# Query weight of a cross-attention kernel loaded in runs of 32 channels and transposed by VectorE instead of TensorE

## What is computed

```python
query = hidden_states @ Wq                 # x: 2 x 2048 x 640, f32
keyt, valt = enc @ Wk, enc @ Wv            # enc: 124 tokens of 384 channels
hs = _mha(query, keyt, valt)
ca_q1 = jnp.einsum('btc,th->bch', ca, Wq_ca)[:, indices, :]   # ca: 4 tokens
ca_hs1 = _mha(ca_q1, residual, residual)   # attends to x itself
ca_hs2 = _mha(ca_hs1 @ Wq, ca @ Wk_ca, ca @ Wv_ca)
out = (hs + ca_hs2) @ Wout + b_out + residual
```

## Time and profile before

| | |
|---|---|
| median of three runs | 768.8 us (767.13 to 770.88) |
| the profiled execution, its own time | 769.75 us |
| its span in the trace | 768.0 us |
| TensorE busy | 725.4 us, 94% of the span |
| VectorE busy | 564.1 us, 73% |
| ScalarE busy | 375.9 us, 49% |
| mean granted TensorE clock | 0.982 of full speed |

### The profile page before, as it was taken

The page is one execution under the profiler, slowest core; times in us unless marked ns, Lnnn a source line. Parts: engine busy times, 40 slices in busy tenths (PEclk is TensorE's granted clock), DMA queues, the critical chain, the costliest instruction groups (busy, mean ns, idle before and its releaser), DMA issues.

```text
span 768.0 us, 12603 instructions
## 1 busy us (share of the span) xinstructions
PE 725.4 (94%) x4693; PEld 677.1 (88%) x4693; DVE 564.1 (73%) x952; ACT 375.9 (49%) x942; POOL 171.4 (22%) x205
## 2 busy tenths in 40 slices
PE   7998999999899996968999999999999999799998
PEld 5978999999788886968899999999978887699997
DVE  3456888888899997436674888888889998656562
ACT  1634544454588962222333544455479994142330
POOL 8024951222100003502210521111110002211220
PEclk9999999999999999888999999999999999899999
DMA  8424353333400046697754334444230005578852
GB/s 275 144 94 124 69 125 90 90 90 90 145 30 1 0 76 157 137 218 183 151 139 101 65 90 109 102 98 94 90 129 2 0 1 128 131 159 188 177 124 74
DMA packets 227021, 82.37 MB, mean 107 GB/s; under 512 B 208324, under 2 KB 210372, under 8 KB 226960
## 3 DMA queue, kind: packets, MB, share of 16 engines
q1 hardware_dynamic: 226960, 81.56, 43.4%
HBM read 50.06 MB, written 31.39 MB: 106 GB/s over the span
## 4 chain that ended last, share of the span: by engine, by line
PE 80%; DVE 8%; SPq 3%; DMA 3%; issue 3%; ACT 2%; POOL 0%; DVEq 0%; POOLq 0%
PE PS L1230 30%; PE PS L1435 13%; PE PS L1418 6%; PE PS L1205 6%; PE PS L1305 6%; PE PS L1336 6%; PE PS L1327 5%; PE PS L1177 2%; SPq L432 2%; PE PS L1142 2%; DMA exT<-p_kept 2%; DVE pT_lo L1047 1%; SPq L479 1%; DVE res L1063 1%; PE PS L1188 1%
## 5 line engine op out<-in xcount | busy, mean ns | idle before, releaser
L1230 PE MATMUL PS<-mm_hi,xT_hi 128*128 128x280 f32 (+3 forms) x480 | 159.5, 332 | 0.0
L890 DVE TENSOR_REDUCE mpart<-PS 128x4 f32<-128x512 f32 x192 | 131.6, 687 | 36.9 <-PE PS L1205 36.7
L1230 PE MATMUL PS<-mm_hi,xT_lo 128*128 128x280 f32 (+3 forms) x480 | 157.4, 328 | 0.0
L1230 PE MATMUL PS<-mm_lo,xT_hi 128*128 128x280 f32 (+3 forms) x480 | 156.5, 326 | 0.0
L560 POOL TENSOR_TENSOR ex<-ex,rinv 128x992 f32<-128x992 f32 x30 | 55.4, 1845 | 201.5 <-DVE rinv L884 201.4
L666 ACT ACTIVATE ex<-PS,neg 128x124 f32<-128x124 f32 x256 | 89.9, 364 | 11.7 <-DVE gs L872 6.4
L1230 PEld LDWEIGHTS PS<-mm_hi,xT_hi 128*128 128x128 f32 x480 | 90.2, 188 | 0.7 <-issue 0.5
L1230 PEld LDWEIGHTS PS<-mm_lo,xT_hi 128*128 128x128 f32 x480 | 90.4, 188 | 0.3
L1230 PEld LDWEIGHTS PS<-mm_hi,xT_lo 128*128 128x128 f32 x480 | 90.3, 188 | 0.3
L754 ACT ACTIVATE oT_hi<-PS 128x256 fp32r<-128x256 f32 x80 | 29.5, 384 | 121.7 <-PE PS L1418 121.1
L608 POOL TENSOR_TENSOR xin<-xin,bias 128x640 f32<-128x640 f32 x32 | 49.8, 1562 | 160.6 <-DMA xin<-in_x 160.6
(11 more groups left out here) (154 smaller groups left out, 1355.9 us busy)
## 6 DMA issues: line engine op xcount, KB each, us to landing
ex_kept<-ex SPq DMA_DIRECT2D x32, 512.0 KB, 2.9
ex<-ex_kept SPq DMA_DIRECT2D x112, 128.0 KB, 3.1
xin<-in_x SPq DMA_DIRECT2D x128, 80.0 KB, 2.9
xin<-in_x SPq DMA_DIRECT2D x32, 320.0 KB, 3.5
out<-res SPq DMA_DIRECT2D x32, 320.0 KB, 2.3
raw_kept<-raw SPq DMA_DIRECT2D x5, 512.0 KB, 2.6
ex<-ex_kept SPq DMA_DIRECT2D x4, 512.0 KB, 3.8
mm_lo<-raw_kept SPq DMA_DIRECT2D x10, 186.0 KB, 4.4
```

What stands on the lines that cost most here:

```text
L890: nc.vector.tensor_reduce(mpart[:, n // 2, :, 2 * (n % 2):2 * (n % 2) + 2, i].rearrange("p s k -> p k s"), PS[:, 6 + N % 2, :].rearrange(" ...
L1230: last = mul(PS[:, slot(T, k), p0:p0 + w], l[:, i % 2, j, :], rr[:, m0:m0 + w], start=(j == 0 and n == 0), stop=(n == 2), skip_group_check ...
```

## The change

The query weight is no longer transposed on TensorE. It is loaded by fifteen transfers, three for each block j of 128 channels of the first axis: each takes 32 channels t, the four groups c of 32 inside the block, all eight heads, and a run of 32 head channels (128 bytes; the third run of a head has 16, so 64 bytes). Each transfer has 32 x 8 x 4 = 1024 pieces. `wq_in` is now `[96, 5, 8, 4, 32]`, and VectorE transposes one block j at a time, 96 partitions x 1024 elements, into `wqT[0:96]`. The unused part of the third run is set to zero by one memset at the start of VectorE's list. Blocks 0 to 2 are transposed before the copies to `kT`, block 3 after step m = 1 and block 4 after step m = 5. The 40 transposes of L1159, the eight copies of L633 and the waits between them go. `wkca` is issued after the three transfers of block 0, and tile 0 of x after all fifteen.

```diff
@@ SP @@
-            for f in range(2):
-                sp.dma_start(wq_in[:, :, f * HALF:(f + 1) * HALF], wq[:, f * HALF:(f + 1) * HALF].rearrange("(j p) n -> p j n", p=P))\
-                    .then_inc(wq_in_s[f], 16)
-                if f == 0:
+            for j in range(KT):
+                rows = wq[j * P:(j + 1) * P, :].rearrange("(c t) (h d) -> t h c d", c=4, h=NH)
+                for d in range(3):
+                    w = min(32, D - d * 32)
+                    sp.dma_start(wq_in[d * 32:(d + 1) * 32, j, :, :, 0:w], rows[:, :, :, d * 32:d * 32 + w]).then_inc(wq_in_s[j], 16)
+                if j == 0:
                     sp.dma_start(wk_in[:, 1], wkca.rearrange("(c p) n -> p c n", p=P)).then_inc(wkca_in_s, 16)
@@ ScalarE @@
-            for h in range(NH):
-                act.wait_ge(wqT_ps, h + 1)
-                nc.scalar.activation(wqT[0:D, h, :], flat(2 * (h % 2))[0:D, 0:H], ACT.Copy).then_inc(wqT_made, 1)
@@ VectorE @@
+            def query_blocks(j):
+
+                dve.wait_ge(wq_in_s[j], 3 * 16)
+                nc.vector.transpose(wqT[0:3 * 32, :, j * P:(j + 1) * P], wq_in[:, j].rearrange("t h c k -> t h (c k)")).then_inc(wqT_made, 1)
+            nc.vector.memset(wq_in[2 * 32:3 * 32, :, :, :, 16:32].rearrange("t j h c k -> t (j h c) k"), 0.0).then_inc(wq_zero, 1)
...
+            dve.wait_ge(wq_zero, 1)
+            for j in range(3):
+                query_blocks(j)
             for m in range(NH // 2):
                 dve.wait_ge(kT_ps, m + 1)
...
                 nc.vector.tensor_copy(ca0[:, 2 * m:2 * m + 2, :], ps[:, :, 0, NK:P]).then_inc(ca0_made, 1)
+                if m in (1, 5):
+                    query_blocks(3 + m // 5)
@@ TensorE @@
             pe.wait_ge(wca_made, 1)
+            pe.wait_ge(wkca_in_s, 16)
             for h in range(NH):
-                if h % R == 0:
-                    pe.wait_ge(wq_in_s[h // R], 16)
-                if h >= 2:
-                    pe.wait_ge(wqT_made, h - 1)
-                if h == 1:
-                    pe.wait_ge(aTm_made, R)
-                for j in range(KT):
-                    last = nc.tensor.transpose(flat(2 * (h % 2))[0:D, j * P:(j + 1) * P], wq_in[:, j, h * D:(h + 1) * D], ident[:, :])
-                last.then_inc(wqT_ps, 1)
-                if h == 0:
-                    pe.wait_ge(wkca_in_s, 16)
                 last = kT_part(h, 1, NK, P)
                 if h % 2:
                     last.then_inc(kT_ps, 1)
+            pe.wait_ge(aTm_made, R)
             for m in range(4 * KT):
                 j, h = m // 4, 2 * (m % 4)
-                if m == 0:
-                    pe.wait_ge(wqT_made, NH)
+                if m % 4 == 0:
+                    pe.wait_ge(wqT_made, max(3, j + 1))
```

More of the change, by code:

```diff
@@ L199, in build @@
             with (nc.sbuf_tensor("wk_in", [P, 2, CT, H], F32) as wk_in,
-                  nc.sbuf_tensor("wq_in", [P, KT, H], F32) as wq_in, nc.sbuf_tensor("wqca_in", [NT, H], F32) as wqca_in,
+                  nc.sbuf_tensor("wq_in", [3 * 32, KT, NH, 4, 32], F32) as wq_in, nc.sbuf_tensor("wqca_in", [NT, H], F32) as wqca_in,
                   nc.sbuf_tensor("v_ca", [B * NT, H], F32) as v_ca):
@@ L327, in build @@
                                                             sem("wout_loaded"))
-        wq_in_s = [sem("wq_loaded0"), sem("wq_loaded1")]
+        wq_in_s, wq_zero = [sem("wq_loaded0"), sem("wq_loaded1"), sem("wq_loaded2"), sem("wq_loaded3"), sem("wq_loaded4")], sem("wq_zero")
         bias_in = sem("bias_loaded")
         wca_ps, wca_made, ctxT_ps, ctxT_made, caT_made = sem("wca_ps"), sem("wca_made"), sem("ctxT_ps"), sem("ctxT_made"), sem("caT_made")
-        kT_ps, kT_made, wqT_ps, wqT_made = sem("kT_ps"), sem("kT_made"), sem("wqT_ps"), sem("wqT_made")
+        kT_ps, kT_made, wqT_made = sem("kT_ps"), sem("kT_made"), sem("wqT_made")
         raw_ps, raw1_made, mmh_made, mml_made, ca0_made = sem("raw_ps"), sem("raw1_made"), sem("mmh_made"), sem("mml_made"), sem("ca0_made")
```

## The result

The changed kernel takes 782.64 us (median of four runs, 781.65 to 784.75), against 769.4 for the kernel before in the same comparison. The ratio is 1.018, with a 95% interval from 1.015 to 1.021: 1.8% slower, where 0.57% faster was forecast. The profiled execution took 781.65 us with a span of 779.9, 11.9 us longer than before.

What follows compares the result with a forecast made beforehand. TensorE's setup chain from keys to folding was taken as the bound: 4.45 us gained there, less 0.1 for the memset, gives 4.35 us, so 764.4 us against 768.8 (0.57% less), range 762.4 to 769.0.

Steps and rivals of the forecast that it cites:

- The tiny products: TensorE between keys and folding: 24 eight-column products stay, taken as 3.5 us, bounded by 2.96 and 4.24.
- the folding: TensorE stage after the tiny products (L1177): begins at 22.44 in place of 26.89, a gain of 4.45 us.
- The memset: Head of VectorE's list: 2.2 us, fits an idle hole of 2.22 us; 0.1 us charged at most.
- the transposes: VectorE's five transposes of the query weight, 1.23 us each, three before the copies to `kT`: cost nothing.
- Block 2: Third query-weight block: lands at 16.9 by the first pace, 1347 pieces a us; last moment 20.5.
- the fast row: Transfer paces in the trace: 1347 pieces a us, taken for the blocks; the slow rows show 778 and 638.
- `wv` and tile 0 of x: Loads queued behind the fifteen transfers: tile 0 lands by 25.5, `wv` by 30.7; wanted at 41.1 and 40.0.
- the rival: TensorE's clock falls after 3.5 us of only eight-column products: costs 1.7 us, 766.1, or twice that; chance 0.14.
- The prediction's own signs of being wrong: VectorE waiting for `wq_in` past 20.5, `ctxT` copy after 5.2, clock below 1.0 between 19 and 30, `wv` wait.
- The rivals of the transfers: Query-weight blocks land late: somewhat, 765.6 or 768.2, chance 0.14; or enough to slow the kernel, 772.1, chance 0.09.
- The slow case: Block 2 lands after 24.97, so VectorE and TensorE stand waiting; at 500 pieces a us 772.1; chance 0.09.
- The gain: Earlier folding, carried to the end nearly in full: 4.45 less 0.1 gives 4.35 us.

Runs made afterwards that it cites:

- the first experiment: Changed kernel with 40 TensorE transposes, results unread, put back between the tiny products: 772.15 us, ratio 1.002 to the kernel before.
- second experiment: Changed kernel with the tiny products moved forward, in pairs of heads between the last full products of the keys: 768.39 us, ratio 0.996 to the kernel before.
- third experiment: Changed kernel with the folding over 128 rows in place of 80, the added rows zero: 767.96 us, ratio 0.997 to the kernel before.
- fourth experiment: Kernel before with only TensorE's order changed, the 40 transposes first and then all 24 tiny products together: 788.76 us, ratio 1.023.
- fifth experiment: Changed kernel with tiny products in pairs of heads and the memset moved later in VectorE's list: 765.44 us, ratio 0.993 to the kernel before.
- the sixth: Changed kernel with the tiny products in two halves, behind head 3's last full product and directly ahead of the folding: 767.07 us, ratio 0.994 to the kernel before.

## Why the prediction was wrong

**The forecast's own steps held.** The tiny products together took 3.38 us (3.5 taken) and the folding began at 22.23 (22.44). The memset took 2.19 us (2.2) and the transposes 1.23 each (1.23). Block 2 landed at about 18.0 (16.9 by the first pace), 2.5 us ahead of its last moment; between the arrivals of blocks 1 and 2 lie 2.06 us, nearer to the fast row than to the slow ones. The margin is not always that wide: with the same transfers, VectorE's third transpose, which waits for block 2, began at 19.16 in the first experiment and 19.05 in the second. `wv` and tile 0 of x kept nobody waiting. The memset was mis-sized in its effect: VectorE's list began 0.42 us later than before, the memset took 2.19 and 0.17 stood idle behind it, so what goes before the first `ctxT` copy ended 2.78 us later, 0.56 more than the hole of 2.22. The copy came at 5.67 and not by 5.2, and the keys began 0.35 us late (6.24 against 5.89), where 0.1 had been charged. That the folding still began within 0.2 us of the forecast is partly luck: the first third of the keys gave 0.44 back.

**The step that failed** is the clock, which the sum put at nothing and the rival at 1.7 us, or 3.4 at most. It cost 16.7. The rival's mechanism was right and its place too: eight-column products for 3.5 us, clock at half behind them. Two things in it were wrong. First its chance of 0.14: "with the tiny products the engine never stops" was taken as speaking against a fall. The runs show that a busy engine is no protection. The profile calls TensorE busy for 3.40 of 3.40 us in 18.80 to 22.20 both before, where the clock stayed up, and after, where it fell 0.7 us later. Second its length. The price of 1.7 us came from a fall that lasted 3.4 us, and behind that fall stood work on all 128 rows. Behind this one stands the folding on 80 rows, and at half rate it never lifted the clock: 34 us. The third experiment isolates that term: the folding alone lost 1.7 us with 128 rows against 16 with 80. That the folding ran at full before was no sign that it could reach full by itself; it only shows that it didn't lose it. The prediction's own signs of being wrong told it: a granted clock below 1.0 between 19 and 30, and a `ctxT` copy later than 5.2, which points at the memset. The Trainium skill, TensorE: Matmul & The Clock Gate, "What's actually happening", has the clock rise again by activity; here the measurement adds that 33 us of unbroken products on 80 rows weren't enough for that (33.52 in the changed kernel, 33.04 in the fourth experiment).

Two slips in the working didn't matter. The 0.34 us for a product of the keys is not the half-rate time: by the pace it is a mean over a stretch that had both levels (fifth experiment). The folding shows the true pair, 0.419 against 0.219, and the 1.7 us follow from the ratio of the clocks and not from 0.34 and 0.21, which would give 1.3. And two thirds of 0.58 with 0.05 make 0.44 for faster, not 0.46.

**The rivals of the transfers** did not occur: the first experiment has them all and loses nothing in the setup. The slow case came true in its sign only, by another mechanism.

**The gain** was carried on about as forecast, once the clock is set apart. In single executions the first scores come 5.2 us earlier (second experiment) or 6.2 (fifth), but 0.84 and 1.30 of that are the luckier first third of the keys: 4.4 and 4.9 remain. In the medians the second shows 2.2 us, the sixth 4.1 and the fifth 5.7. The estimate of the first experiment, made for every run and averaged, takes the half rate out:

| kernel (runs) | mean span | cost of half rate | rest |
|---|---|---|---|
| before, first chip (29) | 769.1 | 15.2 | 753.9 |
| changed (4) | 781.2 | 31.4 | 749.7 |
| 1, transposes kept (10) | 770.6 | 16.3 | 754.2 |
| 2, in pairs (12) | 766.0 | 16.5 | 749.5 |
| 3, over 128 rows (10) | 766.5 | 16.9 | 749.6 |
| 4, before, tiny last (4) | 786.7 | 33.0 | 753.6 |
| before, second chip (12) | 769.6 | 15.1 | 754.5 |
| 5, pairs, late memset (6) | 763.5 | 15.8 | 747.7 |
| 6, in halves (5) | 764.6 | 15.0 | 749.6 |

The rests fall in two groups. The kernels that keep the transposes on TensorE have 753.6 to 754.5, those that lose them 749.5 to 749.7, or 747.7 with the late memset. So the change is worth 4 to 5 us (near 7 with the late memset), where 4.35 was forecast, and the clock took 16 us of half rate in return. The clock's later falls differ from one execution to the next by more than the gain: of the twelve runs of the kernel before on the second chip, the slowest (span 774.1, clock 0.976) has 18.6 us of half rate and the fastest (766.9, 0.984) 12.3. A change of this size needs many runs.

## What to carry to other kernels

When work is taken off TensorE, look at what is left there: narrow products that were harmless between wide ones may form a stretch that costs the clock, though the profile calls the engine busy. Price a fall not by its usual length but by what stands behind it; a stage that uses part of the rows may run at full only because it inherits full. The remedy is free where the order is: spread the narrow products among wide ones (second, fifth and sixth experiments), or give the next stage all rows with zeros (third).

## What the runs showed of the hardware that was not expected

- TensorE's clock fell from 2.4 to 1.2 GHz behind 3.38 us of unbroken eight-column products (three kernels: changed, third and fourth experiment), and stayed up with stretches of 0.80, 1.66 and 1.25 us of them in the profiled executions of others. One unprofiled run with the stretch of 1.25 us had a mean clock of 0.960.
- At 1.2 GHz the folding of 128 x 256 over 80 rows ran unbroken for 33.5 and 33.0 us without the clock rising; the values over 128 rows saw it rise after about 1.4 and 2.3 us. With zeros in the other 48 rows the folding was back at full within 3.4 us of the fall.
- Transfers of 1024 pieces of 128 or 64 bytes, many of them starting at odd multiples of 64 bytes, brought a block of 3072 pieces 2.06 us after the one before it in the changed kernel, which is 1490 pieces a us, and after 2.19 to 3.06 us (1400 to 1000 a us) in the experiments that load it in the same way. The fast row lies among them.
